# A deformable convolution's sampling stage: convolve the image with the nine taps first, then gather, weight and add

## The chip, the cores and the metric

The kernel runs on one core of a Trainium2 chip. The metric is device time in microseconds from the first to the last instruction of that core. An element is 32-bit float unless the text says otherwise. PE is the matrix engine, DVE the vector engine, ACT the scalar engine, POOL the engine that here issues the gathers, SP the queue that issues the plain transfers.

## The reference, cut to what matters

The input is x of shape (32, 64, 56, 56). Four layers follow each other, each adding its result to its input: a convolution pair in hyperbolic space, a quantised pair, a binarised pair, and a deformable convolution. The change touches the last one only (and how its table in DRAM is blanked at the start of the program):

```python
offset  = conv3x3(g, offset_w)                # g = group-normalised x; 18 channels: (dy, dx) for each of 9 taps
for tap k at output pixel (y, x):             # sample position
    sy, sx = y - 1 + k // 3 + dy_k,  x - 1 + k % 3 + dx_k
    patch_k[c] = bilinear(g[c], sy, sx)       # 4 corners, each weight * corner; zero outside the image
y[o]  = sum over c, k of patch_k[c] * deform_w[o, c, k]
attn  = sigmoid(mean(y) + std(y))             # per image and channel, over the pixels
out   = x + y * attn
```

## The kernel before, in words

The program runs its layers one after the other; the deformable layer is `deform_phase` and begins at about 3,730 us. It takes the 32 images in 16 pairs. A pair lies on 128 partitions (2 images x 64 channels) and has 2 x 3136 output pixels, which are 49 tiles of 128 pixels. The 49 tiles are 7 groups of 7; the position of a tile in its group is its slot, and the buffer `g` has one place for each of the 7 slots.

**The table.** For each image the normalised image is turned (`columns`, PE L1888, ACT copy L1820 into `rt`) and stored to DRAM (SP L1752, 2 transfers per pair) so that a table entry (y, x) holds the 64 channels of pixel (y, x) and then those of pixel (y+1, x). Two neighbouring entries, 1 KB in one piece, are the four corners of any sample. Four images have a place in the table, two in use and two being prepared.

**The gathers.** For each tile POOL issues nine indirect transfers (L1786), one per tap. Each brings for 128 pixels, one per partition, the 256 numbers of the four corners. Before it gathers into a slot again, POOL waits for `bank_done` (PE has read the slot's last content) and for `index_ready` (DVE has put the new indices in place).

**A tile's work.** DVE multiplies the right corners by their weights into PSUM (L2046), the left ones in place (L2047) and adds the two (L2049), in three batches of 4, 4 and 1 taps; the weights stand in PSUM, where ACT copies them once a group (L1842). PE turns each tap's 128 x 128 block (L1927) into three PSUM banks, ACT copies these to `corners` (L1852), PE multiplies them with the taps' weights and adds all up over channels, taps and the upper and lower row (18 instructions, L1936), and ACT copies the 64 x 128 result to `big` (L1857).

**What sets the order.** Every engine has its own hand-written program; `around` gives each the same frame. For each pair it takes a group (`turn`), then one part of the preparation of the next pair (a `stage`), then the next group, and so on; the stages are the normalisation, `columns`, the offset convolution in two parts (L1900, ACT copy L1829), and the turning of the offsets (L1915) with the positions, weights and indices on DVE (`positions`). After the seventh group `finish` takes the statistics and writes the pair out. In a group ACT copies the weights of the next group only after the last tile's `big`, and DVE begins no group without them (`w_loaded`).

## Time and profile before

| | |
|---|---|
| median of 3 runs | 16241.07 us (16188.99 to 16253.03) |
| the profiled execution | 16240.73 us, span 16239.1 us |
| first and last gather | 3863.7 and 16170.5 us |
| groups between them | 112 |
| busy, share of the span | PE 52%, weight loads 35%, DVE 40%, ACT 19%, POOL 46% |

The profile was taken on one execution. A row of a group of instructions gives the line, engine, operation and tile, the number of instructions, their busy time in all and the mean of one in ns, and then the engine's idle time before them with what ended it; "remote" there is a release for which the profile names no instruction, "issue" idle time in which the engine waited for nothing that the profile shows. A timeline row gives start, duration, engine, line and, in brackets, the idle time before.

### The profile page before, as it was taken

To read this page: it belongs to the slowest core of one execution; us is meant where nothing else is said; L and a number is where in the kernel's file an instruction comes from. 1 tells how busy PE (TensorE), PEld (TensorE's weight loads), DVE (VectorE), ACT (ScalarE), POOL (GpSimd) and SP (SyncE) were. 2 spreads that over 40 slices of the span, in tenths; PEclk is the share of its full clock that TensorE was granted. 3 is DMA by queue.
4 is the path that set the end of the run, shared out by engine and by line. 5 is a ranking of instruction groups with operands and counts; after the bars stand their busy time and mean duration, and the time that the engine had idled before them with its cause. 6 is when DMAs were issued, how large, how long until landed. Compare 5 with 4: busy or idle time off the path is not lost.

```text
span 16239.1 us, 156068 instructions
## 1 busy us (share of the span) xinstructions
PE 8397.7 (52%) x51639; PEld 5686.8 (35%) x51639; DVE 6489.1 (40%) x13120; ACT 3053.4 (19%) x5214; POOL 7442.3 (46%) x7657
## 2 busy tenths in 40 slices
PE   6897888894435353434344443434343535343433
PEld 2333444483323233323233333333332323233322
DVE  5555656532342433343333343333434242433333
ACT  3433444431111111111111111111111111111111
POOL 0012222223555545555555555555555555555555
PEclk9998999996666666666666666666666666666666
DMA  3231111163232323232323232333323232323232
GB/s 93 78 87 60 55 55 55 52 212 95 85 96 81 101 82 100 82 105 76 106 75 100 83 99 81 100 84 92 96 86 97 84 96 81 100 83 98 81 88 76
DMA packets 503924, 1436.05 MB, mean 88 GB/s; under 512 B 128980, under 2 KB 234196, under 8 KB 474576
## 3 DMA queue, kind: packets, MB, share of 16 engines
q0 software_dynamic: 353344, 970.88, 20.7%
q1 hardware_dynamic: 150032, 458.00, 9.4%
q8 instruction: 328, 5.37, 0.1%
q14 instruction: 220, 1.80, 0.0%
HBM read 1175.46 MB, written 252.90 MB: 88 GB/s over the span
## 4 chain that ended last, share of the span: by engine, by line
another core or an unknown queue 37%; PE 18%; issue 11%; DVE 7%; ACT 2%; DMA 1%; ACTq 0%; DVEq 0%; POOL 0%; SPq 0%
PE e_ps L1936 7%; PE e_ps L1900 5%; PE e_ps L1927 2%; PE e_ps L1915 2%; DVE e_g L2047 2%; ACT e_corners L1852 2%; DVE e_g L2049 1%; PE e_ps L1888 1%; DVE e_sty L2054 1%; DMA out<-e_big 1%; DVE e_x3t L1960 1%; DVE e_w_next L2005 0%; DVE e_big L2067 0%; DVE e_x3t L1964 0%
## 5 line engine op out<-in xcount | busy, mean ns | idle before, releaser
L1786 POOL DMA_INDIRECT e_g<-table_dram,e_index_slots x7056 | 6747.7, 956 | 5689.0 <-PE e_ps L1927 2537.6
L1936 PE MATMUL e_ps<-e_corners,e_w_def 128*64 128x128 f32 x14112 | 2539.4, 353 | 4586.7 <-ACT e_corners L1852 3002.7
L1936 PEld LDWEIGHTS e_ps<-e_corners,e_w_def 128*64 128x64 f32 x14112 | 2221.6, 184 | 4848.3 <-ACT e_corners L1852 3144.6
L1927 PE MATMUL e_ps<-k_ident,e_g 128*128 128x128 f32 x7056 | 1243.3, 324 | 1934.2 <-DVE e_g L2049 1867.2
L2021 DVE COPY e_index_slots<-e_index_now 128x9 uint32<-128x9 uint32 (+1 forms) x784 | 142.8, 183 | 5003.7 <-ACT e_ps L1842 4898.3
L1927 PEld LDWEIGHTS e_ps<-k_ident,e_g 128*128 128x128 f32 x7056 | 930.6, 164 | 2246.4 <-DVE e_g L2049 1952.7
L1857 ACT ACTIVATE e_big<-e_ps 64x128 f32<-64x128 f32 (+1 forms) x784 | 211.9, 270 | 7124.4 <-remote 5947.6
L1852 ACT ACTIVATE e_corners<-e_ps 128x512 f32<-128x512 f32 (+1 forms) x2352 | 1040.4, 489 | 2566.8 <-remote 1313.5
L2049 DVE TENSOR_TENSOR e_g<-e_g,e_ps 128x512 f32<-128x512 f32 (+1 forms) x2352 | 1302.8, 554 | 375.1 <-remote 173.4
L2046 DVE TENSOR_TENSOR e_ps<-e_g,e_ps 128x512 f32<-128x512 f32 (+1 forms) x2352 | 1326.3, 564 | 247.5 <-DVE e_g L2049 99.1
L2047 DVE TENSOR_TENSOR e_g<-e_g,e_ps 128x512 f32<-128x512 f32 (+1 forms) x2352 | 1284.9, 546 | 0.0
L1900 PE MATMUL e_ps<-e_pad,e_w_off 128*64 128x448 f32 x2016 | 901.6, 595 | 231.7 <-issue 225.2
L1200 PE MATMUL c_ps<-c_spad,w_s 128*128 128x448 bf16 x3024 | 614.0, 364 | 7.6 <-ACT c_spad L1072 4.3
L1900 PEld LDWEIGHTS e_ps<-e_pad,e_w_off 128*64 128x64 f32 x2016 | 295.4, 148 | 819.4 <-issue 807.3
L1987 DVE TENSOR_TENSOR e_tmp<-e_ps,e_base 128x450 f32<-128x450 f32 (+1 forms) x32 | 19.8, 618 | 1225.8 <-PE e_ps L1915 1225.8
L2054 DVE BATCH_NORM_STATS2 e_sty<-e_big 64x6 f32<-64x448 f32 x224 | 119.4, 603 | 925.0 <-ACT e_big L1857 925.0
L613 PE MATMUL b_ps<-b_vpad,w_w 64*64 64x392 f32 x4608 | 447.4, 511 | 23.9 <-ACT b_usq L555 12.4
L172 PE MATMUL c_ps<-c_s,k_sel 128*28 128x224 f32 x2240 | 438.3, 355 | 38.2 <-ACT c_s L1015 17.8
L1915 PE MATMUL e_ps<-k_ident,e_x3t 18*128 18x18 f32 (+1 forms) x1600 | 334.7, 353 | 227.7 <-issue 227.1
L613 PE MATMUL a_ps<-a_vpad,w_w 64*64 64x392 f32 x4608 | 439.3, 505 | 7.8 <-DVE a_vpad L781 7.8
L1915 PEld LDWEIGHTS e_ps<-k_ident,e_x3t 18*128 18x128 f32 (+1 forms) x1600 | 342.0, 315 | 224.1 <-issue 221.2
L1578 PE MATMUL d_ps<-d_spad,w_s 128*128 128x224 bf16 x4032 | 403.1, 261 | 26.9 <-ACT d_spad L1550 23.8
(438 smaller groups left out, 8374.3 us busy)
## 6 DMA issues: line engine op xcount, KB each, us to landing
e_g<-table_dram,e_index_slots POOLq DMA_INDIRECT x7056
table_dram<-e_rt SPq DMA_DIRECT2D x32, 1624.0 KB
a_xt<-x_in SPq DMA_DIRECT2D x16, 1568.0 KB
v_dram<-a_vout SPq DMA_DIRECT2D x32, 784.0 KB, 8.5
b_xt<-v_dram SPq DMA_DIRECT2D x16, 1568.0 KB
v_dram<-b_vout SPq DMA_DIRECT2D x32, 784.0 KB, 7.5
c_v2t<-v_dram SPq DMA_DIRECT2D x16, 1568.0 KB
c_xt<-x_in SPq DMA_DIRECT2D x16, 1568.0 KB, 6.5
```

The source lines that it names most:

```text
L172: mm = pe.matmul(out, select[:, j, :], source[:, j * SCH:(j + 1) * SCH], start=(j == 0), stop=(j == NS - 1))
L613: mm = pe.matmul(ps[half * C:(half + 1) * C, CONV[2 * (r % 2) + img], 0:RC], w[img * C:(img + 1) * C, tap, :], tile_window(vpads[parity], ...
L1200: mm = pe.matmul(ps[:, CONV[j % 2], 0:CH], parts[n % 3][:, n // 3, :], window(spad[:, :], j, n // 3), start=(n == 0), stop=(n == 3 * TAPS ...
L1786: pool.indirect_dma_start(out=g[:, slot, tap * CORNERS:(tap + 1) * CORNERS], out_offset=None, in_=table, in_offset=bass.IndirectOffsetOnAx ...
L1852: act.activation(corners[:, taps[0]:taps[-1] + 1, :], ps[:, TURN[bank], 0:len(taps) * P].rearrange("p (k x) -> p k x", x=P), ACT.Copy).the ...
L1900: mm = pe.matmul(ps[0:C, PREP[j % 2], 0:CH], w_o[:, tap, :], window(pad[:, :], j, tap), start=(tap == 0), stop=(tap == TAPS - 1))
L1915: mm = pe.matmul(ps[to:to + hi - lo, PREP[half], col * 2 * TAPS:(col + 1) * 2 * TAPS], x3t[rows, lo:hi], k.ident[rows, rows], start=True, ...
L1927: mm = pe.transpose(ps[:, TURN[tap // 4], (tap % 4) * P:(tap % 4 + 1) * P], g[:, slot, tap * CORNERS:tap * CORNERS + 2 * C], k.ident[:, :])
L1936: mm = pe.matmul(ps[0:C, OUT, 0:P], w_d[:, tap, :], corners[:, tap, :], start=(tap == 0), stop=(tap == TAPS - 1))
L2046: dve.tensor_tensor(half, sides[:, lo:hi, 1, :, :], spread(1), ALU.mult).then_inc(weighted, 1)
L2047: dve.tensor_tensor(left, left, spread(0), ALU.mult).then_inc(weighted, 1)
L2049: dve.tensor_tensor(left, left, half, ALU.add).then_inc(added, 1)
```

## The change

Convolution and sampling are both linear, so the product with a tap's weights can be taken before the sampling. For each tap the pair's images are multiplied with that tap's 64 x 64 weights and the result gets a table of its own, nine per image. A tile is then nine gathers, each from its tap's table, one multiplication of all 36 corners by their weights, and a sum over taps and sides. The sum is taken on PE: 18 matmuls of a 128 x 128 block of `g` with the identity, added up in PSUM. They leave the lower row's part on partitions 0 to 63 and the upper row's on 64 to 127; ACT copies the latter down (`lift`) and DVE adds the two into `big` (`fold`), for slots 0 to 3 and 4 to 6 at a time.

The stage list has now six entries: normalisation, four parts of `project` with the offset convolution, and the positions. `project` takes ten chunks per pair (image 0 or 1, two taps each and the ninth alone); a chunk is 8 runs of up to 4 rows, each run at most 8 matmul calls (two instructions each in 32-bit float) into one of three PSUM banks and one ACT copy into one of two `rt` buffers, and is stored by SP as 2 transfers per tap, 36 per pair in all, 812 KB each. A third chunk's copy waits until the stores of the chunk two before have landed. The weights for DVE are copied a group ahead, into two PSUM banks. POOL waits for `summed`, one signal per tile, in place of `bank_done`. The nine tables of four images are blanked at the start of the program.

```diff
-        corners = s.sb("corners", [P, TAPS, P])
+        upper = [s.sb("upper0", [C, FOLD_A * P]), s.sb("upper1", [C, FOLD_B * P])]
-        rt = s.sb("rt", [W, 2 * (H + 3) * C])
+        rt = [s.sb(f"rt{n}", [P, 2, LAST, C]) for n in range(2)]
+    CHUNKS = [(b, taps) for b in range(2) for taps in ((0, 2), (2, 4), (4, 6), (6, 8), (8, TAPS))]
+    RUNS = [(lo, min(lo + 4, LAST)) for lo in range(0, LAST, 4)]            # LAST = 30
+    PARTS = (((0, 1, 2), (0,)), ((3, 4), (1, 2)), ((5, 6, 7), (3, 4)), ((8, 9), (5, 6)))
+    FOLD_A, FOLD_B = 4, SLOTS - 4
 @block.sync (prepare)
+                    for c, (b, taps) in enumerate(CHUNKS):
+                        sp.wait_ge(rt_ready, n * ROW_STEPS + (c + 1) * len(RUNS))
+                        for tap in range(*taps):
+                            for h in range(2):
 ...
+                                sp.dma_start(dst, src).then_inc(table_stored[c % 2], 16)
 @block.gpsimd
-                        pool.wait_ge(bank_done, (r - 1) * (3 * SLOTS) + (3 * slot + 3))
+                        pool.wait_ge(summed, (r - 1) * SLOTS + (slot + 1))
 @block.scalar
+                def project(n, chunks):
+                    for c in chunks:
+                        lo_tap, hi_tap = CHUNKS[c][1]
+                        need(act, table_stored[c % 2], n * PAIR_STORES + stores_before(c))
+                        for m, (lo, hi) in enumerate(RUNS):
+                            turn_no = c * len(RUNS) + m
+                            act.wait_ge(rows_turned, n * ROW_STEPS + (turn_no + 1))
 ...
+                                           ACT.Copy).then_inc(rt_ready, 1)
+                def lift(r, which):
+                    act.wait_ge(summed, r * SLOTS + (FOLD_A if which == 0 else SLOTS))
+                    act.wait_ge(folded, r * 2 + (which + 1))
+                    width = upper[which].shape[1]
+                    act.activation(upper[which][:, :], ps[C:P, OUT[which], 0:width], ACT.Copy).then_inc(upper_ready, 1)
+                def turn(p, group, first=False, last=False):
+                    if first:
+                        weights(p, 0)
+                    if group < GROUPS - 1:
+                        weights(p, group + 1)
+                    if not first:
+                        lift(r - 1, 1)
+                    lift(r, 0)
 @block.tensor
+                def project(n, chunks):
 ...
+                            if turn_no >= 3:
+                                pause(pe, rt_ready, n * ROW_STEPS + (turn_no - 2), passed)
+                            for y in range(lo, hi):
+                                for h in range(2):
+                                    first = (y + h * HALF_ENTRIES) * PW + 1
+                                    mm = pe.matmul(ps[h * C:(h + 1) * C, PREP[turn_no % 3],
+                                                      (y - lo) * cols:(y - lo + 1) * cols],
+                                                   pad[image, first:first + C], w_def[image, lo_tap * C:hi_tap * C],
+                                                   start=True, stop=True)
+                            mm.then_inc(rows_turned, 1)
 turn:
+                        pe.wait_ge(weighted, r * SLOTS + (slot + 1 + SLOTS))
+                        if place == 0:
+                            pe.wait_ge(folded, r * 2 + (which + 1))
+                        for n in range(2 * TAPS):
+                            mm = pe.matmul(ps[:, OUT[which], place * P:(place + 1) * P],
+                                           g[:, slot, n * 2 * C:(n + 1) * 2 * C], k.ident[:, :],
+                                           start=(n == 0), stop=(n == 2 * TAPS - 1))
+                        mm.then_inc(summed, 1)
 @block.vector (turn)
+                        corners = g[:, slot, :].rearrange("p (n c) -> p n c", c=C)
+                        w = ps[:, WEIGHTS[group % 2], slot * (TAPS * 4):(slot + 1) * (TAPS * 4)]
+                        dve.tensor_tensor(corners, corners, w.unsqueeze(2).broadcast_to([P, TAPS * 4, C]),
+                                          ALU.mult).then_inc(weighted, 1)
+                        if slot in (0, FOLD_A) and not first:
+                            fold(r - 1, group - 1, slot // FOLD_A)
-                around(dve, (normalise, none, none, none, positions), turn, none, finish)
+                around(dve, (normalise, none, none, none, none, positions), turn, none, finish)
 l0_conv_phase, @block.gpsimd (blanking the table)
+                        rows = k.table[b].rearrange("t y x c -> (t y x c)").rearrange("(p r n) -> p r n", p=P, n=part)
+                        pool.dma_start(rows, zeros[:, :].unsqueeze(1).broadcast_to([P, 2 * TAPS, part])
+                                       ).then_inc(filled, 16)
+                        pool.wait_ge(filled, 16 * b + 16)
```

## Rows read from the trace of the kernel before

**Rows 1.** The page, busy time of each engine and its share of the span.
```profile
PE 8397.7 (52%) x51639; PEld 5686.8 (35%) x51639; DVE 6489.1 (40%) x13120; ACT 3053.4 (19%) x5214; POOL 7442.3 (46%) x7657
```

**Rows 2.** The gathers' line: count, ns min/median/max, first and last start.
```profile
L1786 POOL DMA_INDIRECT e_g<-table_dram,e_index_slots x7056: 940/946/4162, 3863.7 to 16170.5; - x196
```

**Rows 3.** Timeline of POOL, one group: start, duration, line, idle before.
```profile
6064.41 0.94 POOL L1786 DMA_INDIRECT e_g<-table_dram,e_index_slots  x1 [39.58 <-PE e_ps L1927]
...
6090.87 0.95 POOL L1786 DMA_INDIRECT e_g<-table_dram,e_index_slots  x1 [4.25 <-remote]
...
6149.65 0.95 POOL L1786 DMA_INDIRECT e_g<-table_dram,e_index_slots  x1 [0.30 <-issue]
6162.84 0.94 POOL L1786 DMA_INDIRECT e_g<-table_dram,e_index_slots  x1 [12.25 <-PE e_ps L1927]
```

**Rows 4.** Timeline of DVE at the turn from one group to the next.
```profile
6094.04 0.28 DVE L2047 TENSOR_TENSOR e_g<-e_g,e_ps 128x128 f32<-128x128 f32 x1
...
6156.39 0.17 DVE L2021 COPY e_index_slots<-e_index_now 128x9 uint32 x1 [61.74 <-ACT e_ps L1842]
...
6157.11 0.68 DVE L2047 TENSOR_TENSOR e_g<-e_g,e_ps 128x512 f32<-128x512 f32 x1
```

**Rows 5.** Timeline of ACT in the same group.
```profile
6089.95 0.27 ACT L1857 ACTIVATE e_big<-e_ps 64x128 f32 x1 [20.27 <-remote]
...
6155.25 0.27 ACT L1857 ACTIVATE e_big<-e_ps 64x128 f32 x1 [20.89 <-remote]
6155.74 0.38 ACT L1842 ACTIVATE e_ps<-e_w_now 128x252 f32 x1 [0.22 <-issue]
```

**Rows 6.** Timeline of PE in the same group.
```profile
6063.44 4.10 PE L1936 MATMUL e_ps<-e_corners,e_w_def 128*64 128x128 f32 x18
...
6069.07 2.18 PE L1936 MATMUL e_ps<-e_corners,e_w_def 128*64 128x128 f32 x18
```

**Rows 7.** The page's groups of instructions (busy us, mean ns, idle before).
```profile
L1936 PE MATMUL e_ps<-e_corners,e_w_def 128*64 128x128 f32 x14112 | 2539.4, 353 | 4586.7 <-ACT e_corners L1852 3002.7
...
L2021 DVE COPY e_index_slots<-e_index_now 128x9 uint32<-128x9 uint32 (+1 forms) x784 | 142.8, 183 | 5003.7 <-ACT e_ps L1842 4898.3
...
L1857 ACT ACTIVATE e_big<-e_ps 64x128 f32<-64x128 f32 (+1 forms) x784 | 211.9, 270 | 7124.4 <-remote 5947.6
...
L1900 PE MATMUL e_ps<-e_pad,e_w_off 128*64 128x448 f32 x2016 | 901.6, 595 | 231.7 <-issue 225.2
...
L1915 PE MATMUL e_ps<-k_ident,e_x3t 18*128 18x18 f32 (+1 forms) x1600 | 334.7, 353 | 227.7 <-issue 227.1
```

**Rows 8.** Matmuls with 64 x 64 weights in an earlier layer, stretch 400 to 1500 us.
```profile
L613 PE MATMUL b_ps<-b_vpad,w_w 64*64 64x392 f32 x4608 | 447.4, 511 | 23.9 <-ACT b_usq L555 12.4 <-issue 6.2 <-DVE b_vpad L781 5.3
```

**Rows 9.** ACT's copies in the stage `columns` of two pairs, and a `big` between.
```profile
5695.81 1.07 ACT L1820 ACTIVATE e_rt<-e_ps 56x512 f32<-56x512 f32 x2 [9.91 <-remote]
...
5702.51 0.59 ACT L1820 ACTIVATE e_rt<-e_ps 56x512 f32<-56x512 f32 x1 [0.28 <-PE e_ps L1888]
...
6391.28 0.27 ACT L1857 ACTIVATE e_big<-e_ps 64x128 f32<-64x128 f32 x1 [42.20 <-remote]
...
8788.75 0.59 ACT L1820 ACTIVATE e_rt<-e_ps 56x512 f32<-56x512 f32 x1 [2.30 <-PE e_ps L1888]
```

**Rows 10.** The line L1820: its instructions, and what its idle time waited for (us, times).
```profile
L1820 ACT ACTIVATE e_rt<-e_ps x224: 578/590/592, 3769.2 to 15010.9; 56x512 f32<-56x512 f32 x112
...
  remote: 120.2, 24
  PE e_ps L1888: 109.3, 181
```

**Rows 11.** The table's stores: issue time in ns on SP (min/median/max), first and last.
```profile
L1752 SPq DMA_DIRECT2D table_dram<-e_rt x32: 358/3544/7145, 3782.1 to 15012.3; - x32
```

**Rows 12.** A stretch with table stores alone: PE, PEld, DVE, ACT, POOL, clock, DMA, GB/s.
```profile
3784.00:3796.00 12.00, 12.00 (x33) 4.35 (x32) 0.00 (x0) 0.58 (x2) 0.00 (x0) 1.00 0.78 188
```

**Rows 13.** DVE's first index copy after `finish`.
```profile
6279.30 0.17 DVE L2021 COPY e_index_slots<-e_index_now 128x9 uint32<-128x9 uint32 x1 [7.22 <-ACT e_ps L1842]
```

More of the change, by code:

```diff
@@ L1708, in around, with stores_before @@
                 for n, stage in enumerate(stages):
-                    with eng.Fori(n, n + 1) as group:
-                        turn(p, group)
+                    turn(p, n, first=(n == 0))
                     stage(p + 1)
-                with eng.Fori(len(stages), GROUPS) as group:
-                    turn(p, group)
+                turn(p, GROUPS - 1)
                 finish(p)
             begin(PAIRS - 1)
-            with eng.Fori(0, GROUPS - 1) as group:
-                turn(PAIRS - 1, group)
-            turn(PAIRS - 1, GROUPS - 1, last=True)
+            for n in range(GROUPS):
+                turn(PAIRS - 1, n, first=(n == 0), last=(n == GROUPS - 1))
             finish(PAIRS - 1)
+        def stores_before(c):
+            return sum(2 * 16 * (hi - lo) for b, (lo, hi) in CHUNKS[c % 2:c:2])
         with nc.Block() as block:
@@ L1828, in offsets, with prepare, stage @@
                         act.wait_ge(off_conv, n * N + (j + 1))
-                        act.activation(x3t[0:OFF_ROWS, chunk(j)], ps[0:OFF_ROWS, PREP[j % 2], 0:CH],
+                        act.activation(x3t[0:OFF_ROWS, chunk(j)], ps[0:OFF_ROWS, OFFSETS, 0:CH],
                                        ACT.Copy).then_inc(off_ready, 1)
+                def prepare(part):
+                    def stage(n):
+                        project(n, part[0])
+                        offsets(n, part[1])
+                    return stage
@@ L1864, in finish @@
                     act.activation(fin[:, 8:10], fin[:, 6:8], ACT.Sigmoid).then_inc(final_a, 1)
-                around(act, (normalise, columns, lambda n: offsets(n, FIRST), lambda n: offsets(n, REST),
-                             lambda n: None), turn, begin, finish)
+                around(act, (normalise, *(prepare(part) for part in PARTS), lambda n: None), turn, begin, finish)
             @block.tensor
@@ L1901, in offsets, with prepare, stage @@
                                            start=(tap == 0), stop=(tap == TAPS - 1))
                         mm.then_inc(off_conv, 1)
+                def prepare(part):
+                    def stage(n):
+                        project(n, part[0])
+                        offsets(n, part[1])
+                    return stage
                 def turn_offsets(n):
                     pe.wait_ge(off_ready, n * N + N)
+                    pe.wait_ge(rt_ready, n * ROW_STEPS + ROW_STEPS)
                     for t in range(PX_TILES):
@@ L1947, in _ @@
                 dve.memset(table_half[:, :], 0.0).then_inc(half_ready, 1)
+                for n in range(2):
+                    dve.memset(fin[:, 2 * n:2 * n + 2], 0.0).then_inc(folded, 1)
+                for slot in range(SLOTS):
+                    dve.memset(sty[:, slot:slot + 1], 0.0).then_inc(weighted, 1)
                 dve.wait_ge(half_ready, 1)
@@ L2007, in positions @@
                     c.end()
-                    pause(dve, table_stored, n * 32 + 32, passed)
+                    for b in range(2):
+                        pause(dve, table_stored[b], n * PAIR_STORES + PAIR_STORES, passed)
                     if isinstance(n, int):
@@ L2027, in switch, with fold, turn @@
                     dve.wait_ge(switched, turn * 3 + 2)
-                def turn(p, group, last=False):
+                def fold(r, group, which):
+                    width = upper[which].shape[1]
+                    dve.wait_ge(upper_ready, r * 2 + (which + 1))
+                    dve.tensor_tensor(at(big, group * (SLOTS * P) + which * (FOLD_A * P), width),
+                                      ps[0:C, OUT[which], 0:width], upper[which][:, :], ALU.add).then_inc(folded, 1)
+                def turn(p, group, first=False, last=False):
                     r = p * GROUPS + group
@@ L2235, in layouts @@
     out["c_base"] = np.stack([y, x], -1).astype(np.float32).reshape(P, -1)
-    index = (pixel // HW * IMAGE_ENTRIES + TX + 1) * ENTRY + 0 * tap
+    index = ((pixel // HW * TAPS + tap) * IMAGE_ENTRIES + TX + 1) * ENTRY
     out["c_index"] = index.astype(np.float32).reshape(P, -1)
```

162 lines of the change are left out of this document (55 added, 107 removed).

## The prediction, on record before the changed kernel ran

> **What bounds the kernel now.** I read the page first. No engine is busy for much more than half of the span [rows 1], so the deformable layer must be waiting. The gathers' line gives its frame: 7056 gathers of 0.945 us, the first at 3863.7 and the last at 16170.5 [rows 2]. That is 12,307 us for 112 groups, 109.9 us a group. In POOL's timeline one gather follows the next after 0.30 us, so 63 of them need 63 x 1.25 = 78.8 us. The other 31 us of a mean group are POOL's gaps: 4.25 and 12.25 us inside a group, 39.6 us after a stage [rows 3].
>
> DVE is no bound. It spends some 35 us on the seven tiles of a group and then waits 61.74 us for ACT's copy of the weights [rows 4]. ACT makes that copy right behind the last `big` [rows 5]. And `big` waits, 20.27 and 20.89 us, for something that is "remote". But PE ended that slot's last sum (2.18 us of work, 6069.07 to 6071.25) 18.7 us before ACT moved at 6089.95 [rows 5, 6]. What lies between is POOL's burst from 6064 to 6086.6: POOL's last gather ended, and 3 us later ACT went on, and POOL itself at 6090.87. So while POOL gathers, PE's signals arrive late. I read this as the kernel's real bound: 5947.6 us of waiting in line L1857, and 4898 us in DVE's wait for the weights [rows 7]. The lockstep (weights after the last `big`, DVE's tiles after the weights, POOL after PE) turns it into idle POOL.
>
> **The change part by part.** The profiled execution took 16240.73 us, the median is 16241.07, so times of the profile stand for the median.
>
> *Gathers.* The count stays, 7056 x 1.25 = 8,820 us.
>
> *A tile on DVE.* Two multiplications and an addition in three batches become one product of 128 x 2304. DVE takes 0.68 us for 512 elements and 0.28 for 128 [rows 4], 1.04 ns an element, so 2.6 us a tile in place of about 5.0, and 18 us a group. It had a cover of 62 us and gains nothing directly.
>
> *A tile on PE.* Turning (9 instructions), ACT's three copies and 18 instructions become 36 instructions of 128 columns. 18 take 4.10 us at the lower clock and 2.18 at the higher [rows 6], so 8.2 or 4.4 us (0.228 or 0.121 us an instruction), under the 11.25 us in which POOL fills a slot. ACT's corner copies go, with their 3002.7 us of waiting on PE's line [rows 7]; they lay beside POOL. Instead ACT has two `lift`s a group.
>
> *Weights a group ahead.* The copy waits no more for the last `big`, so DVE's 61.7 us go. What is late next is `summed`: POOL needs the slot's last tile summed, 79 us after it gathered it. If the signal passes at once, it is 60 us early.
>
> *A plain group when signals are held.* POOL runs until it needs a held signal, stops, and the signal passes: the gap of 4.25 us at 6090.87 is this very event [rows 3]. I take 4.3 us a group (between 0, if signals pass, and 12.25 x 2, if `folded` makes PE wait behind a second held signal).
>
> *The projection.* Per pair ten chunks, 80 runs, in place of 14 turns. A two-tap chunk has 60 calls, 120 instructions of 128 columns; one after another they take 120 x 0.121 = 14.5 us. Earlier instructions of 64 x 64 weights and 392 columns take 97 ns each (447.4 us / 4608), less than a third of what 128 columns' 0.121 us implies, so they run side by side [rows 8]. The change alternates two halves of the array, hence half, 7.3 us. ACT's copy is 0.59 us plus 0.28 [rows 9], 8 x 0.88 = 7.0 us a chunk. I take 0.88 us a run, bounds 0.88 to 1.8. The offset convolution stays, 901.6 / 112 = 8.05 us a chunk, 8.6 with ACT's copy; turning the offsets stays at 334.7 / 16 = 20.9 us [rows 7].
>
> Here held signals bite, since PE and ACT take turns at every run. `columns` shows it: under gathers a copy waited 9.91 us in one pair and 2.30 in another, when POOL is quiet 0.28 [rows 9]; the line waited 24 times for "remote", 120.2 us, 5.0 us each [rows 10], so 5.6 us a signal with the copy. The bounds are 2.9 (the 2.30) and 5.6; I take their middle, 4.2. A stage stands in PE's program behind a group's last tile. POOL goes on for about 79 - 10 = 69 us (it takes about 10 from the last tile's gathers to its sum), in which 69 / 4.2 = 16 signals pass. Then POOL stops, because the next group's sums stand behind the stage, and the rest of the stage goes at full pace while POOL is idle:
> - part 1 (24 runs, 1 offset chunk): 8 x 0.88 + 8.6 = 15.6
> - part 2 (16, 2): 17.2
> - part 3 (24, 2): 8 x 0.88 + 17.2 = 24.2; part 4 (16, 2): 17.2
>
> Together 74.2 us. To each comes 8.6 us until POOL runs again: release 3.3, the first sum 4.4, restart 0.9, so 34.4. Turning the offsets (20.9 us, no turns with ACT) and the normalisation fit into 79. With three plain groups, 12.9, a pair loses 121.5 us.
>
> *Table stores.* Bytes per pair grow from 3.33 to 29.9 MB. The stretch in which only the old stores move has 188 GB/s [rows 11, 12]: 29.9 MB / 188 = 159 us, 17.7 us a two-tap chunk. For pair 0 this is open: chunks ready by about 3,780, so the first gather comes at about 3,945 in place of 3,864, +80 us (a little more for blanking 61.6 MB instead of 6.8 in the first layer, which 10 us should cover). For the others it lies beside gathers, which move 131 KB per 1.25 us, 105 GB/s; 83 remain, 29.9 MB / 83 = 360 us, within the five groups that are there. SP issues 36 transfers at a median of 3.5 us [rows 11], 126 us, beside four groups.
>
> The Trainium skill has, in "SBUF — State Buffer", § Who interferes with whom, the sentence "PE and ACT never wait on anyone." The two 20 us waits of ACT in this trace speak against it as far as signals go; by the rule the time would be that of rival A.
>
> *Positions and finish.* DVE's positions now stand behind the sixth group; POOL has a whole group of indices, 79 us of cover. After `finish` DVE's first index copy waited 7.22 us [rows 13]; POOL's gathers ahead cover it. Cost 0; without the cover 16 x 7.2 = 120 us.
>
> **The sum.** First gather 3,945, gathers 8,820, tail 65 (68 now, last gather to end [rows 2]): 12,830. Held signals 15 x 121.5, and 7 x 4.3 = 30 in the last pair: 1,850. Together 14,700 us. Unknowns: at 5.6 us a signal 12 pass, and 4 x 4 x 0.88 = 14 us a pair come on top, +210; at 2.9 us 24 pass, so all runs do and in parts 2 and 4 an offset chunk or two as well, 40 us a pair less, -600; PE unshared in the projection (16 to 32 leftover runs x 0.92 us, +220 to 440); second stops in plain groups (3 x 8 us, +360). Own range 13,900 to 15,600.
>
> **The rivals.**
>
> *A: no signal is late any more.* The hold might belong to the many signals of the old tile (seven that PE and ACT exchange) or to its transposes, and go with them. Then every stage fits under 79 us: 3 x 7 + 8.6, or 3 x 7.3 + 17.2 = 39 us, plus seven sums of 4.4 = 31, 70 in all. Time 12,830 to 12,950, if nothing at all is late. For it: the signals to PE come at once, some of PE's do too, and the projection has three banks where `columns` had two, so that a late signal leaves two in reserve. If they pass three at a time, no more than the 4.3 us a group are left and it is 13,300. Against it: `columns` has no tiles' transposes in it and lost 5.0 us a signal all the same [rows 10]. Chance 0.32.
>
> *B: the forecast.* Chance 0.42.
>
> *C: slower. In a stage nothing passes while gathers run.* A burst is now 79 us long, against 22 to 34 before; and behind a pair's first stage `big` waited 42.20 us for one signal [rows 9]. If PE gets on in a stage only once POOL has stopped, whole stages are open: 24 x 0.88 + 8.6 = 29.7, 31.3, 38.3, 31.3, each + 8.6; the turned offsets 29.5, plain groups 8.6, ACT's wait for the stores of the chunk two before 26, and a second stop of 4.3 in five groups 21.5: 251 us a pair, 12,830 + 15 x 251 + 30 = 16,625. It is slower than before from (16,241 - 12,830) / 15 = 227 us a pair on. For it: the 9.91 and the 42.20 us; also that 80 runs a pair stand where 14 stood. Against it: "remote" waits of 5.0 us each are the rule in the stage. Chance 0.16.
>
> *D: the stores are what is late.* A chunk's stores share with the gathers, 3.33 MB / 83 = 40 us instead of 17.7, and the third chunk of a part waits for the first's. In parts 1 and 3 that keeps PE some 20 to 30 us longer in the stage than B has it, beyond POOL's stop: +2 x 25 us a pair, 15,450; the stop then ends with a store's landing. Chance 0.10.
>
> PE at its lower clock throughout would be 49 x 8.2 + 10 x 14.5 + 7 x 16 + 42 = 700 us of work a pair, 16 x 700 + 3,945 = 15,150; PE busy this much is not likely to stay there, since it rose from 4.10 to 2.18 us a sum within one burst [rows 6].
>
> **How the numbers follow.** B, being likeliest, gives the time, 14,700. The range takes in A's lower end, 12,800, and ends at 16,300, short of C's point; outside are about 0.15 above and 0.03 below. Slower by over 0.5% (16,322; 0.5% is about what a measurement of this kernel tells from no change) is the greater part of C, 0.15; within 0.5% 0.04, where the costs come out near 227 us a pair; faster 0.81.
>
> **What the changed profile would show.** POOL's timeline: right if a plain group repeats after 83 us with one gap of about 4 us, and groups after parts 1 to 4 have gaps of 24 to 33 us; A if all repeat after 79, C if gaps are over 38 after each stage and over 29 after the turned offsets. ACT's copies of the projection: waits of 2 to 5 us under gathers and near 0.3 after POOL has stopped; in A 0.3 throughout; in D long waits on a table store. DVE: the wait of 61.7 us for the weights gone, one product of 2.6 us a tile. PE: 36 instructions in 4.4 us. The first gather at 3,945. The forecast is wrong if first gather and gather pace are off, if POOL's gaps end on DVE or a DMA, or if PE's signals arrive at once.

## The result and the profile after

The changed kernel takes 17214.8 us (median of 4 runs, 17179.55 to 17218.7) against 16221.17 us (median of 4, the three of before and one more): the ratio is 1.061, 95% interval 1.058 to 1.064. It is slower by 6%, where 14,700 us had been forecast.

The page's busy times and its group for the gathers:

```profile
PE 11034.0 (64%) x76103; PEld 8223.7 (48%) x76103; DVE 4895.4 (28%) x7081; ACT 2461.9 (14%) x3358; POOL 7471.5 (43%) x7656
...
L1797 POOL DMA_INDIRECT e_g<-table_dram,e_index_slots x7056 | 6783.1, 961 | 6660.0 <-DVE e_index_slots L2054 3085.2
```

The line of the gathers and that of DVE's product, with first and last start:

```profile
L1797 POOL DMA_INDIRECT e_g<-table_dram,e_index_slots x7056: 942/949/4201, 3955.4 to 17165.0; - x196
...
L2078 DVE TENSOR_TENSOR e_g<-e_g,e_ps x784: 2533/2544/2555, 3968.4 to 17167.8; 128x2304 f32<-128x2304 f32 x196
```

What [rows 1, 2, 7] showed of before has moved as the sum said, except in one place: DVE has a quarter less to do (6489 to 4895 us), the first gather is 92 us later, each gather costs the same, but POOL's idle time rose. The groups take (17165.0 - 3955.4) / 112 = 117.9 us, not 109.9.

POOL's timeline around one stop of each kind, to be read beside [rows 3]: a signal that is late, and the end of a stage.

```profile
7127.44 0.95 POOL L1797 DMA_INDIRECT e_g<-table_dram,e_index_slots  x1 [5.50 <-remote]
...
7169.98 0.94 POOL L1797 DMA_INDIRECT e_g<-table_dram,e_index_slots  x1 [31.56 <-DVE e_index_slots L2054]
```

From 6664.6 to 7501.7 us one pair passes: 837 us, of which 551 are gathers. Six stops at the ends of groups take 212 us (45.0, 33.8, 52.8, 31.6 behind the four parts of the projection, 31.6 behind the turned offsets, 17.7 behind the end of the pair), fifteen short ones of 2.6 to 9.1 us the other 73.

PE's timeline in the burst that began at 7169.98. It had no stop and no wait for data in it, since 7 tiles stood ready:

```profile
7164.80 14.67 PE L1964 MATMUL e_ps<-k_ident,e_g 128*128 128x128 f32 x129
7179.88 0.50 PE L1964 MATMUL e_ps<-k_ident,e_g 128*128 128x128 f32 x3 [0.41 <-issue]
...
7186.96 0.60 PE L1964 MATMUL e_ps<-k_ident,e_g 128*128 128x128 f32 x2 [1.81 <-issue]
...
7189.81 0.57 PE L1964 MATMUL e_ps<-k_ident,e_g 128*128 128x128 f32 x1 [1.04 <-issue]
...
7199.59 0.37 PE L1964 MATMUL e_ps<-k_ident,e_g 128*128 128x128 f32 x1 [2.43 <-issue]
...
7207.99 11.37 PE L1964 MATMUL e_ps<-k_ident,e_g 128*128 128x128 f32 x79 [0.33 <-issue]
```

For the first 10 us of the burst PE goes at full speed. Then single instructions stand between gaps of "issue", which are close to multiples of 0.7 us. POOL's last gather of the burst ended at 7203.5, and at 7208 PE is quick again. So PE itself gets hardly an instruction through, which the prediction had not seen. The signals are late as well. The instruction at 7189.81 is the last of the group's fourth sum and ended at 7190.37. ACT's `lift` and POOL's next gather both waited for this sum alone, and moved 18 us later:

```profile
7208.26 0.59 ACT L1869 ACTIVATE e_upper<-e_ps 64x512 f32<-64x512 f32 x1 [42.04 <-remote]
```
```profile
7209.03 0.95 POOL L1797 DMA_INDIRECT e_g<-table_dram,e_index_slots  x1 [5.51 <-remote]
```

Counted over the whole trace (36 instructions a sum, none missing), POOL stopped 341 times. 245 of these stops end on "remote" and take 1,164 us; in every one the sum that POOL waited for had ended 3.2 us before or more, 15.4 us in the median. The other 96 take 3,215 us, and in 90 of them POOL moves 0.9 us after the sum ends: there it was PE's work that was late.

The same is in the trace of before, where turning the offsets falls under gathers. I had not looked at this stretch:

```profile
6009.27 3.81 PE L1915 MATMUL e_ps<-k_ident,e_x3t 18*128 18x18 f32 x17
6013.94 0.18 PE L1915 MATMUL e_ps<-k_ident,e_x3t 18*128 18x18 f32 x1 [0.86 <-issue]
6016.75 0.18 PE L1915 MATMUL e_ps<-k_ident,e_x3t 18*128 18x18 f32 x1 [2.63 <-issue]
```

### The profile page after: what moved, and what is told of

Its sections match the earlier page's. It is cut to its first block, busy times and chain, and to the rows that moved or that the text cites. A ratio compares the mean times of both kernels' runs of the same rounds, so it can differ in the third digit from the quotient of the medians.

```text
span 17217.1 us, 189765 instructions
## 1 busy us (share of the span) xinstructions
PE 11034.0 (64%) x76103; PEld 8223.7 (48%) x76103; DVE 4895.4 (28%) x7081; ACT 2461.9 (14%) x3358; POOL 7471.5 (43%) x7656
## 4 chain that ended last, share of the span: by engine, by line
PE 30%; issue 22%; another core or an unknown queue 17%; DVE 3%; DMA 3%; SPq 1%; POOL 1%; ACT 1%; DVEq 0%; ACTq 0%; POOLq 0%
PE e_ps L1964 17%; PE e_ps L1916 8%; PE e_ps L1928 5%; DMA table_dram<-e_rt 2%; SPq L1764 1%; DVE e_g L2078 1%; POOL e_g L1797 1%; DVE e_x3t L1992 1%; DVE e_sty L2091 1%; DMA e_tmp<-x3s_dram 1%; DMA out<-e_big 0%; PE e_ps L1950 0%; DVE e_big L2104 0%; DVE e_x3t L1996 0%
## 5 line engine op out<-in xcount | busy, mean ns | idle before, releaser
L1964 PE MATMUL e_ps<-k_ident,e_g 128*128 128x128 f32 x28224 | 4523.1, 309 | 4552.1 <-issue 3734.4
L1964 PEld LDWEIGHTS e_ps<-k_ident,e_g 128*128 128x128 f32 x28224 | 4090.3, 221 | 4975.9 <-issue 4654.4
L1916 PE MATMUL e_ps<-e_w_def,e_pad 64*64 64x128 f32 x19200 | 2093.4, 388 | 798.6 <-issue 699.6
L1916 PEld LDWEIGHTS e_ps<-e_w_def,e_pad 64*64 64x64 f32 x19200 | 1829.2, 217 | 1082.8 <-issue 1079.2
L2078 DVE TENSOR_TENSOR e_g<-e_g,e_ps 128x2304 f32<-128x2304 f32 x784 | 1992.3, 2542 | 48.4 <-DMA e_g<-table_dram,e_index_slots 48.4
L2066 DVE TENSOR_TENSOR e_big<-e_ps,e_upper 64x512 f32<-64x512 f32 x224 | 137.7, 615 | 6216.2 <-ACT e_upper L1869 6006.1
L1834 ACT ACTIVATE e_rt<-e_ps 128x512 f32<-128x512 f32 (+2 forms) x1280 | 662.3, 530 | 3883.5 <-PE e_ps L1916 2215.2
L2054 DVE COPY e_index_slots<-e_index_now 128x9 uint32<-128x9 uint32 x784 | 133.7, 171 | 2508.6 <-DMA e_g<-table_dram,e_index_slots 2491.4
L1202 PEld LDWEIGHTS c_ps<-c_spad,w_s 128*128 128x128 bf16 x3024 | 298.4, 100 | 313.0 <-issue 35.4
L1580 PEld LDWEIGHTS d_ps<-d_spad,w_s 128*128 128x128 bf16 x4032 | 386.6, 96 | 43.1 <-issue 23.5
```

The source lines that it names most:

```text
L1202: mm = pe.matmul(ps[:, CONV[j % 2], 0:CH], parts[n % 3][:, n // 3, :], window(spad[:, :], j, n // 3), start=(n == 0), stop=(n == 3 * TAPS ...
L1580: mm = pe.matmul(ps[:, n % 2, 0:SCH], parts[t % 3][:, t // 3, :], every_other_row(spad[b][:, :], j, t // 3), start=(t == 0), stop=(t == 3 ...
L1834: act.activation(rt[c % 2][:, 0:hi_tap - lo_tap, lo:hi, :].rearrange("p t y c -> p y t c"), ps[:, PREP[turn_no % 3], 0:width].rearrange("p ...
L1916: mm = pe.matmul(ps[h * C:(h + 1) * C, PREP[turn_no % 3], (y - lo) * cols:(y - lo + 1) * cols], pad[image, first:first + C], w_def[image, ...
L1964: mm = pe.matmul(ps[:, OUT[which], place * P:(place + 1) * P], g[:, slot, n * 2 * C:(n + 1) * 2 * C], k.ident[:, :], start=(n == 0), stop= ...
L2078: dve.tensor_tensor(corners, corners, w.unsqueeze(2).broadcast_to([P, TAPS * 4, C]), ALU.mult).then_inc(weighted, 1)
```

## The experiments

**Theory 1**: while gathers follow each other closely, each other engine gets only about one instruction a gather through, once a reserve is used up; a pause of POOL gives the reserve back. The changed kernel has 3,190 PE instructions a pair (28,224 + 19,200 + 2,016 + 1,600 over 16) in place of 1,661 (21,168 for the tiles, 1,792 for `columns`, 2,016 and 1,600), so it loses. **Theory 2** is the prediction's: only signals are late, and PE itself runs at full speed. **Theory 3**: the gathered bytes get in the way of PE's reading. Ratios below are to the kernel before, timed on the same chip beside each group of kernels: 16,232 us beside e1, 16,250 beside e4, e5 and e6, 15,939 beside e7, e8, e10 and e11, and 16,228 beside e12, e13, e14 and e16. All but the last of these are single executions, and 15,939 is 1.7% below the others, so ratios to it can be 2% too high. The kernels too were run once each, but for e12.

**m1_streams: PE, ACT and DVE beside gathers, nothing else.**
```diff
+ POOL:  for m in range(63): gather(m)                 # phase 1; other phases vary this
+ PE:    for m in range(300): matmul(ps, a, b)         # 600 instructions, no data from the gathers
```


> A program of its own that leaves the whole computation out (its output is zeros). Eleven phases, one after the other; in most of them POOL issues 63 gathers of 9-tap kind (128 entries of 1 KB at random places) back to back while PE works through 600 matmul instructions that read nothing of what is gathered and signal only once, at the end. Phase 0: PE alone. 1: with gathers. 2: bf16, 600 instructions. 3: 16 columns instead of 128. 4: gathers of 256 bytes an entry. 5: a small memset and its wait after each gather. 6: plain transfers in place of gathers. 7: DVE busy as well. 8: 200 small ACT copies under gathers, no PE. 9: 300 small DVE copies, no PE. 10: 60 calls of 512 columns. Theory 1 (while gathers follow each other closely, PE gets through only one instruction in about 2 us, after a reserve of some 80, whatever the instruction is): phase 0 takes 600 x 0.121 = 73 us or less; in phases 1, 2, 3 PE is at full speed for some 10 us and then has gaps of multiples of 0.7 us until POOL has ended; phase 6 has no gaps. Theory 2 (only the signals are late): PE runs at full speed in every phase. Theory 3 (the bytes written to SBUF get in the way of PE's reading): phase 4 is faster than 1, and phase 3 differs from 1. Phases 5 and 7 tell whether a less dense stream of gathers gives PE free; I expect yes, since in the changed kernel's trace PE is quick where DVE is busy.

Each row is a stretch: its length, then busy time and instructions of PE, PE's loads, DVE, ACT and POOL, granted clock, DMA share, GB/s. In order: PE alone; phases 1 (f32), 2 (bf16), 3 (16 columns), 4 (256 bytes an entry), 5 (a small memset after each gather, waited for), 6 (plain transfers), 7 (DVE busy), and phase 10 (instructions of 512 columns) in two halves, each of half of its gathers.

```profile
0.00:77.00 77.00, 69.84 (x601) 69.65 (x602) 5.18 (x7) 0.00 (x0) 0.20 (x4) 1.00 0.01 1
77.10:155.70 78.60, 23.29 (x131) 20.19 (x130) 0.00 (x0) 0.00 (x0) 59.67 (x63) 0.59 0.36 104
219.40:301.20 81.80, 14.96 (x128) 9.08 (x126) 0.00 (x0) 0.00 (x0) 59.57 (x63) 0.55 0.35 100
336.60:415.10 78.50, 23.26 (x127) 25.77 (x127) 0.00 (x0) 0.00 (x0) 59.54 (x63) 0.52 0.36 104
524.60:606.10 81.50, 23.87 (x117) 20.55 (x118) 0.00 (x0) 0.00 (x0) 59.44 (x63) 0.56 0.13 25
668.50:755.50 87.00, 57.51 (x257) 45.34 (x256) 0.00 (x0) 0.00 (x0) 70.16 (x126) 0.61 0.33 94
799.00:866.00 67.00, 67.00 (x600) 66.95 (x600) 0.00 (x0) 0.00 (x0) 0.00 (x0) 1.00 0.35 126
866.40:933.00 66.60, 66.60 (x598) 66.60 (x598) 65.73 (x26) 1.13 (x1) 56.02 (x25) 1.00 0.17 48
...
1226.50:1266.50 40.00, 36.79 (x80) 15.94 (x81) 0.00 (x0) 0.00 (x0) 30.26 (x32) 0.95 0.35 102
1266.50:1305.00 38.50, 13.76 (x14) 3.85 (x14) 0.00 (x0) 0.00 (x0) 27.41 (x29) 0.52 0.36 102
```

Under 63 gathers PE gets 117 to 131 instructions through in 79 us, whether they are f32 or bf16, 128 or 16 columns wide, and whether the gathers move 104 or 25 GB/s; 600 take 67 us beside plain transfers of 126 GB/s. Theory 3 falls, and so does theory 2 as the whole story, as there was one signal at the end. That signals are late too, as seen above, m1 does not touch. In phase 7 DVE was busy with products of two operands in SBUF, each gather took 2.29 us instead of 0.95, and PE was free. Phase 10 shows what the first stretch at full speed is: 80 instructions of 512 columns got through in 40 us, where 92 of 128 columns had in 11. The reserve is a number of instructions, not a time.

Two other causes can be looked up in the trace. Loading of code is not it: the queues that bring code moved 48 packets in the whole program (packets, MB, share of the DMA engines),

```profile
q8 instruction: 38, 0.62, 0.2%
q14 instruction: 10, 0.08, 0.0%
```

and two of them came in phase 1, of 16,384 and 8,192 bytes, in 1.31 and 0.31 us. The number of packets is not it either: the gathers of phase 1 made 38 a us, the plain transfers of phase 6 made 69.

ACT and DVE, in phases 8 and 9, with a wait for their own last copy each time, are held up too. DVE's timeline early and late in one burst, and ACT's in the other:

```profile
1130.00 1.22 DVE L114 COPY m_z<-m_z 128x64 f32<-128x64 f32 x5
...
1172.52 0.20 DVE L114 COPY m_z<-m_z 128x64 f32<-128x64 f32 x1 [1.21 <-DVE m_z L114]
1173.92 0.20 DVE L114 COPY m_z<-m_z 128x64 f32<-128x64 f32 x1 [1.21 <-DVE m_z L114]
```
```profile
1043.32 0.26 ACT L94 ACTIVATE m_e<-m_f 128x64 f32<-128x64 f32 x1 [1.14 <-ACT m_e L94]
1044.72 0.26 ACT L94 ACTIVATE m_e<-m_f 128x64 f32<-128x64 f32 x1 [1.14 <-ACT m_e L94]
```

One copy in 1.40 us, where it was one in 0.25. DVE got 148 copies through before that, ACT only 18: its phase came 2.7 us after other gathers, DVE's 46 us after. So the reserve seems to be common to the engines and to need quiet to come back; that is a reading, not shown by itself. In the kernels ACT and DVE issue few instructions and PE tens of thousands, which is probably why it is PE that suffers.

**m2_pauses: how much rest gives PE back.**
```diff
+ after every `every` gathers:  pool.memset(q[:, 0:width], 0.0), waited for
```


> A program of its own that leaves the whole computation out. Ten phases, in each 63 gathers on POOL and 600 f32 matmul instructions on PE that need nothing of them. POOL pauses with memsets of its own: phase 0 0.9 us after every 9 gathers, 1: 1.9 us after 9, 2: 3.9 us after 9, 3: 3.9 us after 18, 4: a memset of 64 columns after each gather, not waited for, 5: 256 columns after each, 6: 512 columns after each, 7: 768 columns after every 3, 8: 3.9 us after 27, 9: none. Theory 1 (each other engine gets about one instruction a gather once a reserve of some 80 is used up, and the reserve comes back only when POOL pauses): phase 9 about 150 PE instructions in 79 us; phase 2 keeps PE near full speed, since a burst of 11 us doesn't use the reserve up; phases 0 and 1 in between; phases 5 and 6 free PE as well, at 15 to 35 us more of POOL. If it is not pauses but the mere share of time in which POOL gathers that counts, phases 0, 4 and 7 (nearly the same share) are alike.

The same view without ACT's column, eight of the ten phases: a memset of 0.76 us after every 9 gathers, of 1.56 us after 9, of 3.2 us after 9, of 3.2 us after 18, of 0.17 us after each (not waited for), of 0.75 us after every 3, of 3.2 us after 27, none. PE had 600 instructions to do, so x599 and x600 mean that it was not held up.

```profile
8.00:91.10 83.10, 33.42 (x153) 27.95 (x152) 0.00 (x0) 64.39 (x69) 0.59 0.34 98
148.90:240.00 91.10, 71.38 (x465) 65.75 (x464) 0.00 (x0) 69.12 (x70) 0.83 0.31 90
258.40:355.80 97.40, 72.49 (x600) 69.86 (x599) 0.00 (x0) 78.70 (x70) 0.92 0.29 84
359.70:451.00 91.30, 62.59 (x386) 56.53 (x385) 0.00 (x0) 69.20 (x66) 0.73 0.31 90
478.40:564.60 86.20, 29.80 (x143) 23.68 (x143) 0.00 (x0) 70.40 (x126) 0.59 0.33 95
...
836.60:933.10 96.50, 67.88 (x599) 67.69 (x597) 0.00 (x0) 74.93 (x84) 0.85 0.30 85
935.70:1023.90 88.20, 35.00 (x154) 29.74 (x154) 0.00 (x0) 66.03 (x65) 0.56 0.32 93
1075.30:1153.90 78.60, 21.81 (x126) 19.27 (x126) 0.00 (x0) 59.70 (x63) 0.60 0.36 104
```

1.56 us after 9 gathers cost POOL 12.5 us and let through 465 instructions in place of 126; 0.76 us after 9 cost 4.5 and bring only 27. The length of one rest does not decide it: 3.2 us after every 27 gathers gave 154, and 0.75 us after every 3 gave all. Nor does the order in which POOL rests matter much: where 63 gathers take 78.6 to 88.2 us PE gets 126 to 154 instructions, at 91 us 386 and 465, and from 96.5 us on all. What counts is how closely the gathers follow each other on average, with a steep step between 88 and 96.5 us. (m1's phase 5, 257 instructions at 87 us, lies off this order.)

**e1_half_sum: 18 instead of 36 instructions a tile.** It leaves half of the corners out of the sum.
```diff
-                        for n in range(2 * TAPS):
+                        for n in range(0, 2 * TAPS, 2):
```


> The changed kernel with 9 of the 18 identity matmuls a tile: half of the corners are left out of the sum. 784 x 18 = 14,112 matmul instructions fewer, the same number of signals, gathers, stores and copies. Theory 1 (PE's instructions are slowed one by one while gathers run): the plain groups, 120 us now, fall to near POOL's 79 plus 5 to 15, and the whole by 1,500 to 3,000 us, to 14,200 to 15,700. Theory 2 (late signals, each 4 to 6 us): no more than 784 x 2.2 us of PE's own work, most of it hidden, so within 2% of 17,215.

Measured 16,676 us, ratio 1.027. Outside what both theories said: 540 us came, far more than theory 2's hidden work would give but a third of theory 1's least. **e14_wide_project** took most of the projection's instructions away, with products that belong to wrong pixels and taps, and left columns, copies, signals and stores as they were:
```diff
-                            for y in range(lo, hi):
-                                for h in range(2):
+                            for h in range(2):      # one call of (hi - lo) * cols columns
```


> The changed kernel with two projecting calls of up to 512 columns a run in place of eight of 128 (the products then belong to wrong pixels and taps; columns, copies, signals and stores stay the same). 19,200 instructions become about 5,120. Theory 1 (the number of PE's instructions under gathers): the stages' stops shrink, 880 instructions a pair fewer at 0.2 to 2.5 us each, part of them in reserve: 700 to 2,000 us off 17,215, so 15,200 to 16,500. If PE's columns count, or the turns with ACT (80 signals a pair, unchanged), it stays within 2% of 17,215.

16,847 us, ratio 1.038, 370 us less, just below what the rival to theory 1 allowed (within 2%) and far from theory 1's 15,200 to 16,500: again a miss. Both traces show why. In the changed kernel a stage hardly moves under gathers: most of it is done in the stop behind the last burst. One burst and one such stop of the same pair, same columns as above:

```profile
7088.40:7121.90 33.50, 16.28 (x98) 14.26 (x98) 10.89 (x9) 0.00 (x0) 25.55 (x27) 0.65 0.35 102
...
6740.90:6785.90 45.00, 42.01 (x312) 34.17 (x312) 3.71 (x5) 11.56 (x22) 0.00 (x0) 0.61 0.73 193
```

98 instructions in a burst of 33.5 us, 312 in a stop of 45. Under gathers the number of instructions counts, in a stop PE's columns do. e14 kept the columns, and its stops after the four parts are 38.4, 28.3, 45.3 and 27.3 us in place of 45.0, 33.8, 52.8 and 31.6: 24 us a pair, 15 x 24 = 360. e1 kept the stages and lost short stops, about one a group instead of two. A third kernel, with sums of 16 columns (e2), gave no time; that columns do not count under gathers rests on phases 3 and 10 of m1.

**e5_dve_sum: the sum on DVE, one PE instruction a tile.**
```diff
-                        for n in range(2 * TAPS):
-                            mm = pe.matmul(ps[:, OUT[which], ...], g[:, slot, ...], k.ident[:, :], ...)
+                        pe.transpose(ps[:, OUT[which], ...], red[:, slot, :], k.ident[:, :]).then_inc(summed, 1)
+                        dve.tensor_reduce(red[:, slot, 0:C], g[:, slot, :].rearrange("p (n c) -> p c n", c=C),
+                                          mybir.AxisListType.X, ALU.add).then_inc(reduced, 1)
```


> The changed kernel with the sum over taps and sides on DVE (one reduction of 128 x 2304 to 128 x 64 a tile) and only one transposing matmul a tile on PE in place of 36 instructions; POOL waits for DVE's reduction in place of PE's sum; ACT copies four or three tiles at once to big, and lift and fold go. Everything is computed. PE has 35 x 784 = 27,440 instructions fewer, the projection's 19,200 stay. Theory 1 (PE's instruction count under gathers decides): the plain groups run at POOL's pace, 79 to 85 us; the stages still hold PE up, so 13,700 to 15,700 us. Rival (late signals of PE, whatever their number): POOL has no wait on PE any more, but DVE waits for the transposes a group later; gaps stay as they are, near 16,700.

16,436 us, ratio 1.011: less than the changed kernel's, above the forecast. Groups without a stage's end did come to POOL's pace, one stretch of 400 us has no stop at all. But under such a stretch the stage stands nearly still, and the stop behind it is longer:

```profile
7253.00:7448.00 195.00, 27.30 (x101) 15.40 (x102) 95.94 (x53) 6.37 (x8) 147.72 (x156) 0.50 0.38 112
7448.20:7522.50 74.30, 49.18 (x425) 39.95 (x425) 7.73 (x5) 17.54 (x33) 0.04 (x1) 0.60 0.49 130
```

101 instructions in 195 us, then 425 in 74. A kernel in which POOL stops less gives PE less: this ate the gain.

**e4_slot_pause, e7_after_pause3: the changed kernel with rests for POOL.**
```diff
                         gather(slot)
+                        for m in range(4):                                        # e4
+                            pool.memset(still[:, :], 0.0).then_inc(rest, 1)       # 512 columns, 0.53 us
+                            pause(pool, rest, ..., passed)
```


> The changed kernel with four memsets of 512 columns on POOL, each waited for, after every slot's nine gathers, about 3 to 4 us of pause a slot: 784 x 3.5 = 2,700 us more work on POOL. Theory 1 (PE's instructions are held up by back-to-back gathers, and a pause gives them back): faster all the same, 15,000 to 16,500 us, plain groups near 7 x 14.8 = 104 us in place of 120, and PE's isolated matmuls with gaps of 0.7 us or multiples gone from the tiles. Rival (POOL is idle because of the order of waits, and PE is slow for a cause of its own): the pauses come on top, 18,000 to 20,000 us.

> The changed kernel with a memset of 768 columns (0.87 us) on POOL after every third gather, waited for. In the program of streams this spacing freed PE altogether (598 instructions in 66 us) and 63 gathers took 96.5 us in place of 78.6. Theory 1: plain groups near 97 us, PE with no gaps of 0.7 us; PE needs 456 instructions a group on average, 55 to 100 us, so 112 x 97 to 105 = 10,900 to 11,800, with the 4,010 around it 14,900 to 15,800 us. If signals of PE are late for another reason the 18 us a group come on top: over 17,500.

e4: 15,622 us, ratio 0.961. 1,652 us of memsets were added to POOL, with their waits 3.3 us a slot, and the changed kernel became 9% faster. POOL's stops of over 1.35 us fell from 4,353 to 160 us in all, and those that end on "remote" from 226 to one: the rest takes away both the slow instructions and the late signals, and does not tell them apart. PE's sums stand in one piece again, and wait for DVE only:

```profile
7003.44 6.74 PE L1968 MATMUL e_ps<-k_ident,e_g 128*128 128x128 f32 x36 [9.44 <-DVE e_g L2082]
7018.05 6.29 PE L1968 MATMUL e_ps<-k_ident,e_g 128*128 128x128 f32 x36 [7.87 <-DVE e_g L2082]
```

e7: 16,181 us, ratio 1.015, more than expected: PE was free (160 us of stops here too), but the rest with its wait cost 1.27 us or more three times a slot, and POOL set the pace at 109 us a group.

**The same on the kernel before.** e6 has one part of the change (and its groups written out one by one, as in the changed kernel), e11 only the rest (two memsets of 864 columns a slot), e10 both; e8 is e5 with it.
```diff
+                        if slot == SLOTS - 1 and group < GROUPS - 1:      # e6, e10
+                            weights(r + 1, group + 1)                     # ahead of the last big
```


> The kernel before with one part of the change alone: ACT copies the next group's weights right after the last tile's corner copies, ahead of that tile's big, and the groups are written out one by one as in the changed kernel. The wait of 61.7 us of DVE for the weights was put down to the late signal of the last sum. If the weights alone kept the engines in step, the 20 us of this wait go in each of 112 groups: 14,000 to 15,000 us. By theory 1 PE needs 27 x 7 = 189 instructions a group and gets about 80 in a burst and one in 2.5 us behind that, so most of the time stays: 15,500 to 16,300 us.

> The kernel before with nothing but the 1.9 us on POOL after every slot. DVE still waits for the weights after the last big, but that big no longer waits 20 us. Theory 1: group 110 us now; the 20 us wait goes, 13 us come: 15,300 to 16,300 us, faster or the same although POOL has 1,600 us more to do. Rival: 112 x 13 on top, 17,500 us or more.

> The kernel before with the weights ahead (e6) and the same 1.9 us on POOL after every slot. Theory 1: its gaps on late signals (4 to 6 us, 20 to 35 us at a group's end) shrink, groups near 95 us: 14,400 to 15,200 us, against 15,700 without the pauses. Rival (the gaps are the order of waits): 112 x 13 us come on top, 17,000.

> The kernel with the sum on DVE, with two memsets of 864 columns (1.9 us and their waits) on POOL after every slot. In the program of streams bursts of nine with 1.9 us between let through 463 PE instructions in 91 us; this kernel needs 1,475 a pair, 211 a group. Theory 1: POOL hardly ever stops on its own and sets the pace, 91.5 us a group: 4,010 + 112 x 91.5 = 14,260, up to 14,700 with stops behind the longest stages. Rival (DVE with its reduction of 4.0 us a tile, or the stores, set the time in e5): near 16,400 as before, or more.

e6: 15,697 us, ratio 0.966, as theory 1 said. e11: 14,947, ratio 0.938, better than expected: nothing but rest for POOL. e10: 14,933, 0.937: with it, the weights ahead bring nothing more, since POOL runs almost without stops (157 us in e11, where the kernel before had 3,507) at 13.8 us a slot. e8: 15,038, 0.943, above the forecast because from the last gather of a slot to the next one it is 2.9 us and not 1.9. In e11 the wait of ACT's `big` for "remote", 5947.6 us before [rows 7], is 1622.2:

```profile
L1862 ACT ACTIVATE e_big<-e_ps 64x128 f32<-64x128 f32 (+1 forms) x784 | 213.3, 272 | 3380.1 <-remote 1622.2
```

**Half of the rest: e12 (e6), e13 (e5) and e16 (before), one memset of 864 columns a slot.**

> The kernel before with the weights ahead and one memset of 864 columns (0.84 us, some 1.6 us from gather to gather) on POOL after every slot in place of two. With two POOL never stopped for anyone, 13.8 us a slot. If one is enough, 12.7 us a slot: 3,935 + 784 x 12.7 = 13,900 us. In the program of streams 1.0 us after nine gathers let through only 151 instructions in 83 us, and this kernel needs 237 a group: then POOL stops again and it is 14,500 to 15,500. I expect 14,300 to 14,900, and less than the kernel before at any rate.

> The kernel with the sum on DVE and one memset of 864 columns after every slot in place of two. 211 PE instructions a group: if one pause is enough 4,010 + 784 x 12.7 = 13,970, else POOL stops behind the stages, 14,500 to 15,500.

> The kernel before with one memset of 864 columns after every slot and no other edit. With two it was 14,947. Between 14,300 (one is enough, the lockstep costs something) and 15,800 (the pause is too short and signals of PE are late again).

e12 was timed four times: 14,531 us (14,349 to 14,558), ratio 0.893, interval 0.887 to 0.898. e13 is 14,688 (0.905) and e16 14,753 (0.909). All three are as expected: the rest is short enough to pay, though POOL stops again here and there. e12 computes everything, in the old order of things, and beats both kernels:

```profile
7044.89 0.84 POOL L1791 MEMSET e_still<- 128x864 f32 x1
7046.78 0.95 POOL L1785 DMA_INDIRECT e_g<-table_dram,e_index_slots  x1 [1.04 <-issue]
```

## Why the prediction was wrong

- *Gathers*: 7056 x 1.25 held. First gather 3,945 forecast, 3955.4 measured; tail 65 and 52.
- *A tile on DVE*: 2.6 forecast, 2.54 measured; the wait for the weights of 61.7 us is gone, as said.
- *A tile on PE*: this step failed first. "8.2 or 4.4 us, under the 11.25 us in which POOL fills a slot" took PE's speed from rows that lay in POOL's stops or in the first 10 us of a burst. Behind these it is an instruction in 1.4 to 2.8 us. In one burst of 33.5 us PE did 98 instructions, not three tiles (108) and a stage on top.
- *Held signals*: late signals are real, and stop POOL 245 times here: 73 us a pair in short stops, where the forecast had 12.9. But they are the smaller part. That PE's instructions are slowed as well stood in the trace of before as "issue" gaps in L1915. A price per signal (4.3 us a group, 4.2 us a run) made 36 instructions a tile look as cheap as 27. Forecast 121.5 us a pair, measured 837 - 551 = 286, of which 212 are the six long stops.
- *The stages*: this step failed too, and costs most. "69 us ... in which 16 signals pass" gave the stage 69 us under gathers. In fact the group's seven sums, 252 instructions, use up the burst: ACT's first copy of a part comes 8 to 20 us before POOL stops, and 1 to 5 runs are through by then (in one part none), not 16. The four stops, forecast at 24 to 33 us, are 45.0, 33.8, 52.8 and 31.6.
- *PE's clock in the stops*: the forecast took 0.121 us an instruction, the higher clock. What is left of a part runs at the lower one in all stops: 19 runs take 31 us in the stop of 45.0 us, forecast 8 runs and 7 us. Full runs are 1.71 us apart there and 0.87 in the preparation of pair 0, where the granted clock was 1.00. ACT's copy in the stop and in pair 0, then the stretches around them (length, PE, PE's loads, DVE, ACT, POOL, granted clock, DMA share, GB/s):
```profile
6748.94 0.60 ACT L1834 ACTIVATE e_rt<-e_ps 128x512 f32<-128x512 f32 x1 [1.11 <-PE e_ps L1916]
3814.48 0.60 ACT L1834 ACTIVATE e_rt<-e_ps 128x512 f32<-128x512 f32 x1 [0.28 <-PE e_ps L1916]
```
```profile
6745.00:6757.00 12.00, 12.00 (x117) 12.00 (x115) 0.00 (x0) 4.55 (x8) 0.00 (x0) 0.50 0.77 197
3813.00:3819.00 6.00, 6.00 (x125) 6.00 (x121) 0.00 (x0) 4.25 (x8) 0.00 (x0) 1.00 0.81 211
```
  So 107 ns an instruction at 0.50 and about 50 at 1.00, where 128 x 128 weights take 228 and 121 [rows 6] (granted clock 0.50 and 1.00 in its two rows): the halving that the forecast took for the projection held, at either clock. The bound of 1.8 us a run came true by another cause than the one given for it. PE was held up before each of these stops; that this is why the clock was low there fits m1 (1.00 alone, 0.52 to 0.59 held up) but was not tested.
- *Turned offsets*: "fit into 79" put them at nothing; their stop is 31.6 us.
- *Table stores*: nearly hidden, as said. ACT waited for them 33 times, 206.9 us, and 182 of these lie in POOL's stops, two of 6 us a pair; with three banks PE had work meanwhile and stood for 2.0 us in the one at 6757.
- *Rivals*: C was nearest in size, 251 us a pair and 16,625 us, and in its sentence that nothing passes in a stage while gathers run; its reason, a longer burst that holds a signal, leaves out that PE's instructions are slow. A is refuted as long as POOL gathers without rest. The sentence of the Trainium skill ("SBUF — State Buffer", § Who interferes with whom) that PE and ACT wait on no one stands among rules on SBUF's ports. Taken as a rule for overlapping work, m1 contradicts it: 131 instructions in 78.6 us against 600 in 67. Whether they wait at a port of SBUF no run shows.

What in the chip is shared is open. It is not the bytes, the packets, the operands, PE's columns, the loading of code or PE's own semaphores; gathers in close succession are in every case, and plain transfers alone in none. Nor is it tested whether the recording of instructions takes part in it: every execution here has a recorded span and clock.

## What to carry over

Where an engine issues indirect transfers back to back, count the other engines' instructions under them and not their time: here some 70 to 150 at full speed and then one in 1.4 to 2.8 us. Resting POOL for 0.8 to 2.1 us every nine gathers more than paid for itself. An idle time named "remote" asks for the producer's own timeline: how long before the release its last instruction ended, and whether there are gaps named "issue" before it. A duration taken from a profile belongs to its clock; look at the granted clock where the work will lie.

## What the runs showed that was not expected

- Every engine is held up, not PE alone: DVE and ACT come down to one small copy in 1.40 us.
- Adding 0.8 to 2.1 us of useless work to POOL per slot made each of four kernels faster: 17,215 to 15,622 (four times 0.53 us), 16,228 to 14,753, 16,436 to 14,688, and 15,697 to 14,531. Only the second pair was timed side by side.
- Gathers are as quick under DVE's product in the changed kernel (0.95 us, 621 of them) as without it. There the weights stand in PSUM; in m1 both operands stood in SBUF, and a gather took 2.29 us.
